# Click-rate tower on one core: adds and G products moved a tile back, gathers spread over four tiles, the last products regrouped

## The chip, the cores and the metric

The kernel runs on one core of a Trainium2 chip. TensorE (PE) multiplies, VectorE (DVE) and ScalarE (ACT) scale and add, GpSimd (POOL) builds small matrices and issues DMAs, SyncE (SP) only issues DMAs. The metric is the time of one execution on the device, in microseconds (us). Everything is fp32; the largest products are split into three products of rounded parts (hi and lo).

## What is computed

For 512 samples, 39 rows of 16 numbers are gathered from 39 tables. Three interaction layers of 128 rows follow, each summed over the 16 numbers, and then a small dense network:

```python
def _cin_layer(X0, Xi, W, b):
    Wr = W.reshape(H, F0_, Fi)
    return jnp.einsum('hjk,bjd,bkd->bhd', Wr, X0, Xi) + b[None, :, None]
X0 = embedded_features          # 512 x 39 x 16, the gathered rows
for W, b in Ws:                 # three layers
    Xi = _cin_layer(X0, Xi, W, b)
    res.append(Xi.sum(axis=2))
z = jnp.concatenate(res, axis=1)
h = jnp.concatenate([z, dense_ctx], axis=1)       # 3 x 128 + 16 = 400
h = jnp.maximum(h @ W_top1 + b_top1, 0.0)         # 512
h = jnp.maximum(h @ W_top2 + b_top2, 0.0)         # 256
y = h @ W_top3
```

## The kernel before

The 512 x 16 pairs of sample and number are 8192 columns. They are cut into 16 groups (0 to 15) of 512 columns (32 samples), and a group into 4 tiles of 128 columns; there are 64 tiles.

**The first layer of a group** is made one group ahead of its use. DVE multiplies rows of X0 (`form_pairs`, L653, seven times for a group, at chunk positions p = 6, 10, ... 30 of the group before) and PE multiplies these pairs with weights (`pair_product`, L394, five positions later, so at p = 11, 15, ... 35). PE also turns the group's X0 round (`transpose_x0`, L402, at p = 8, ahead of whose chunk it waits for the group's X0 to have been loaded). ACT adds the bias and rounds (L542, L551), DVE makes the rest (L660).

**The second layer** is the bulk of the work. For each tile PE makes ten chunks (`t_chunk`, three products each: L426, L427, L428; the tenth is narrower). ACT (L567) or DVE (L671) scales each chunk by the tile's column of X0 into `prod`. So a group has 40 positions p = 10 x tile + chunk. A tile's 24 slots of `prod` are then folded in half by an accumulating DMA of POOL (`fold`, L346), issued in the following tile, and DVE adds the rest in four steps (`sum_over_j`, L703) into x2, at chunks 1, 3, 5 and 7 of the tile that is BEHIND = 2 tiles later. One tile later again PE multiplies x2 with `diag` (`g_product`, L411), and ACT copies the result into G (`copy_g`, L556). POOL makes `diag` of each tile (`diagonal`, L334) once the tile before is scaled.

**The gathered rows** take a long way. POOL computes the indices of a group (`index`, L317) and issues ten indirect DMAs (`gather`, L324) into one half of `emb`. When all ten have landed, SP stores them to device memory (L245), waits, loads them as X0 (L255), waits, copies them inside SBUF (`rep`, L259, three DMAs), waits, and issues the loads of the factors that `form_pairs` multiplies (`factors`, L268 three DMAs, then L273 six). In its loop SP runs `factors(g)` and then `x0_of(g + 1)`. `factors(g)` is issued around the start of group g - 1, whose positions form the pairs of group g. So the store, load and copy of group g + 2 stand in group g, and its pairs are formed in group g + 1.

POOL's gathers of a group g + 2 are issued in program order between the folds. Before the change, nine of the ten stand in tiles 1 to 3 of group g - 1 and the tenth in tile 0 of group g.

**The end.** The last three G products follow the loop (tiles 61, 62, 63 of 0 to 63). Tile 63 has its fold on DVE (`fold_last`, L685). Between them stand the products of the first dense layer (`first_layer`, L471): four with `z0` of 128 rows and four with the 16 rows of dense_ctx, in turn. Then come nine products of the third layer (L491), four of `first_layer` with G, the split products (L502, L503, L505), and the rest of the dense network, which waits for the activation of z2 (L629).

## Time and profile before

| | us |
|---|---|
| median of 3 runs | 673.68 (673.07 to 673.69) |
| the profiled execution, its time | 672.67 |
| its span, from first to last instruction | 670.6 |
| PE busy in the span | 641.9 (96%) |
| DVE, ACT, POOL busy | 521.2, 488.3, 361.1 |
| mean granted clock of TensorE | 0.995 |

The profiled execution lies 1.0 us below the median of the runs, and 2.1 us of it lie outside the span. A group takes 36 us. Group 0 starts at 44.4 us, group 7 at 295.5 us, group 8 at 331.5 us, and the last tile ends at about 612 us; the rest is the end.

### The profile page before, as it was taken

Reading aid. Unit: us, or ns where it says so; the run is one execution under the profiler, and the core shown is the slowest. Engines: PE = TensorE matmul, PEld = TensorE weight load, DVE = VectorE, ACT = ScalarE, POOL = GpSimd, SP = SyncE. Lnnn points to the kernel's source line nnn. Section 1 sums busy time; section 2 is a strip of 40 time slices with the busy share of each in tenths; the row PEclk is TensorE's granted clock in tenths of the full one; section 3 lists DMA queues with packets and bytes.
Section 4 is the critical chain, followed back from the end, with each engine's and each line's share of the span. In section 5 each row is a group of like instructions: output and inputs, shape, how many; then the busy total and the mean of one; then the engine's idle time right before and its main releaser. Section 6 shows DMA issues by size and latency. Waiting matters only on the chain.

```text
span 670.6 us, 11899 instructions
## 1 busy us (share of the span) xinstructions
PE 641.9 (96%) x2516; PEld 461.4 (69%) x2516; DVE 521.2 (78%) x1478; ACT 488.3 (73%) x1692; POOL 361.1 (54%) x308
## 2 busy tenths in 40 slices
PE   0689999999999999999999999999999999999998
PEld 0246777777777777777777777777777777785483
DVE  0346888878888888888888878888888888897590
ACT  1137877778787868787877878787868787897293
POOL 6878766575656565755666675656575221121000
PEclk9799999999999999999999999999999999999999
DMA  6457687767676777667667767676777657567100
GB/s 225 60 92 168 112 183 133 173 131 162 124 160 128 159 150 163 142 134 155 139 144 134 167 130 161 124 160 129 160 150 162 142 102 178 126 122 215 31 1 0
DMA packets 61944, 91.05 MB, mean 136 GB/s; under 512 B 34599, under 2 KB 38548, under 8 KB 61671
## 3 DMA queue, kind: packets, MB, share of 16 engines
q0 software_dynamic: 14192, 51.02, 42.0%
q1 hardware_dynamic: 47734, 39.85, 21.2%
q8 instruction: 6, 0.10, 0.1%
q14 instruction: 12, 0.09, 0.0%
HBM read 10.59 MB, written 1.28 MB: 18 GB/s over the span
## 4 chain that ended last, share of the span: by engine, by line
PE 91%; POOL 3%; DMA 3%; issue 2%; SPq 1%; ACT 0%; DVE 0%; ACTq 0%; POOLq 0%
PE t_bank L426 22%; PE t_bank L427 21%; PE t_bank L428 21%; PE x_bank L394 14%; PE small_bank L411 5%; POOL emb L324 3%; PE t_bank L491 1%; PE t_bank L471 1%; PE t_bank L502 1%; PE t_bank L503 1%; PE t_bank L514 1%; PE t_bank L505 1%; DMA emb<-in_table,idx 1%; PE x0t_bank L402 1%; DMA emb_scratch<-emb 1%
## 5 line engine op out<-in xcount | busy, mean ns | idle before, releaser
L567 ACT ACTIVATE prod<-t_bank,x0t 128x128 f32<-128x128 f32 x1472 | 417.5, 377 | 114.6 <-PE t_bank L428 109.3
L671 DVE SCALAR_TENSOR_TENSOR prod<-t_bank,x0t,prod 128x128 f32<-128x128 f32 x1024 | 287.9, 343 | 80.1 <-PE t_bank L428 75.8
L426 PE MATMUL t_bank<-w_hi,x_hi 128*128 128x512 f32 (+1 forms) x640 | 307.5, 480 | 0.6 <-DVE x_lo L660 0.3
L427 PE MATMUL t_bank<-w_lo,x_hi 128*128 128x512 f32 (+1 forms) x640 | 247.8, 387 | 0.0
L428 PE MATMUL t_bank<-w_hi,x_lo 128*128 128x512 f32 (+1 forms) x640 | 247.0, 386 | 0.0
L324 POOL DMA_INDIRECT emb<-in_table,idx x160 | 211.8, 1324 | 48.5 <-issue 46.8
L334 POOL TENSOR_TENSOR diag<-x0t,mask 128x320 f32<-128x320 f32 x64 | 87.8, 1372 | 195.4 <-DVE prod L671 97.7
L426 PEld LDWEIGHTS t_bank<-w_hi,x_hi 128*128 128x128 f32 x640 | 120.2, 188 | 54.7 <-issue 29.7
L427 PEld LDWEIGHTS t_bank<-w_lo,x_hi 128*128 128x128 f32 x640 | 120.5, 188 | 47.1 <-issue 25.3
L428 PEld LDWEIGHTS t_bank<-w_hi,x_lo 128*128 128x128 f32 x640 | 120.1, 188 | 24.2
L703 DVE TENSOR_TENSOR prod<-prod 128x768 f32<-128x768 f32 (+2 forms) x192 | 117.4, 611 | 6.0 <-DMA prod<-prod 5.7
L394 PE MATMUL x_bank<-pairs,w_pair 117*128 117x512 f32 x224 | 114.6, 594 | 2.7 <-DVE pairs L653 1.9
L653 DVE TENSOR_TENSOR pairs<-shared 117x512 f32<-117x512 f32 x96 | 65.5, 682 | 6.8 <-DMA shared<-rep 6.8
L346 POOL DMA_DIRECT2D prod<-prod x63 | 60.5, 961 | 0.0
L394 PEld LDWEIGHTS x_bank<-pairs,w_pair 117*128 117x128 f32 x224 | 41.8, 190 | 15.6 <-DVE pairs L653 6.3
L411 PE MATMUL small_bank<-diag,x 128*128 128x320 f32 x128 | 45.0, 433 | 0.0
L556 ACT ACTIVATE G<-small_bank 128x320 f32 (+1 forms) x64 | 29.1, 454 | 4.8 <-PE small_bank L411 4.8
L448 PE MATMUL t_bank<-w_pair 117*128 117x512 f32 x20 | 13.2, 816 | 16.3 <-DVE w_pair L726 16.3
L411 PEld LDWEIGHTS small_bank<-diag,x 128*128 128x128 f32 x128 | 23.9, 188 | 6.8 <-issue 0.8
L534 ACT ACTIVATE x0t<-x0t_bank 128x39 f32<-128x39 f32 x64 | 13.8, 221 | 10.7 <-PE x0t_bank L402 9.2
L542 ACT ACTIVATE x<-x_bank,bias 128x512 f32<-128x512 f32 x16 | 11.4, 715 | 13.2 <-PE x_bank L394 13.2
L625 ACT ACTIVATE w_hi<-G 128x512 fp32r<-128x512 f32 x20 | 12.6, 632 | 11.5 <-PE t_bank L505 10.5
(73 smaller groups left out, 242.8 us busy)
## 6 DMA issues: line engine op xcount, KB each, us to landing
prod<-prod POOLq DMA_DIRECT2D x63, 768.0 KB, 7.1
shared<-rep SPq DMA_DIRECT2D x96, 234.0 KB
shared<-rep SPq DMA_DIRECT2D x48, 78.0 KB
emb<-in_table,idx POOLq DMA_INDIRECT x160
G<-in_w SPq DMA_DIRECT2D x1, 2496.0 KB
rep<-rep SPq DMA_DIRECT2D x28, 78.0 KB
rep<-emb_scratch SPq DMA_DIRECT2D x20, 78.0 KB
prod<-in_w SPq DMA_DIRECT2D x1, 1536.0 KB, 7.1
```

The source lines that it names most:

```text
L324: pool.indirect_dma_start(out=emb[:, half, i * D:(i + 1) * D], out_offset=None, in_=table, in_offset=bass.IndirectOffsetOnAxis(ap=idx[:, h ...
L334: pool.tensor_tensor(diag[:, slot, :, :], x0t[:, slot, :].unsqueeze(2).to_broadcast([P, J1, TB]), mask[:, :].unsqueeze(1).to_broadcast([P, ...
L346: pool.dma_start(prod[:, slot, 0:HALF, :].rearrange("p j h -> p (j h)"), prod[:, slot, HALF:, :].rearrange("p j h -> p (j h)"), accum_op=A ...
L394: pe.matmul(x1_bank[:, :], w_pair[:, b * H:(b + 1) * H], pairs[:, b % 2, :], start=b == 0, stop=b == BLOCKS - 1).then_inc(pair_mm, 1)
L411: pe.matmul(small_bank[:, 0:TB * J1], x2[:, slot % 2, :], diag[:, slot, :, :].rearrange("p j b -> p (j b)"), start=True, stop=True).then_i ...
L426: pe.matmul(acc, hi, w1_hi[:, cols], start=True, stop=False)
L427: pe.matmul(acc, hi, w1_lo[:, cols], start=False, stop=False)
L428: pe.matmul(acc, lo, w1_hi[:, cols], start=False, stop=True).then_inc(t_mm, 1)
L567: last = act.activation(prod[:, s, SLOT[c] + u, :], t_bank[c % T_BANKS][:, u * H:(u + 1) * H], ACT.Copy, scale=x0t[:, s, j:j + 1])
L653: dve.tensor_tensor(pairs[:, b % 2, :], first, rep[0:PAIRS, half, :] if b == 0 else second[:, k, :], ALU.mult).then_inc(pair_ready, 1)
L671: last = dve.scalar_tensor_tensor(unit, t_bank[c % T_BANKS][:, u * H:(u + 1) * H], x0t[:, s, j:j + 1], unit, ALU.mult, ALU.add)
L703: dve.tensor_tensor(out, left, right, ALU.add).then_inc(summed, 1)
```

## The change

BEHIND becomes 3: the adds of a tile come three tiles behind it and its G product four, now after chunk 0 of a tile (it was after chunk 2). In the last tile DVE adds two tiles (60 and 61), PE makes one more G product after chunk 7 (tile 60), and ACT copies it. After the loop tile 63 (folded by DVE) now comes ahead of tile 62 (folded by DMA). The ten gathers of group g + 2 now all stand in group g: 3, 3, 2 and 2 of them in its four tiles; those that were issued one group earlier are gone from there. The 16-row weights and dense_ctx are loaded into four strips of 32 partitions each, so SP issues eight small DMAs in place of two, and the four dense products use a tile position each and stand together between the last two G products. One product of `first_layer` with G moves behind the split products.

The core of the diff:

```diff
-BEHIND = 2
+BEHIND = 3
-GATHERS_EARLY = 9
-INDEX_TILE = 1
-G_AT = 2
+GATHERS_OF_TILE = [(0, 3), (3, 6), (6, 8), (8, GATHERS)]
+G_AT = 0
 G_COPY_AT = 5
+LAST_G_AT = 7
+LAST_G_COPY_AT = 9
...
-            sp.dma_start(wt1[0:D, 3, :], top1[3 * P:, :]).then_inc(wt1_loaded, 16)
-            sp.dma_start(dense[:, :], dense_t).then_inc(wt1_loaded, 16)
+            for m in range(M1):
+                strip = slice(m * STRIP, m * STRIP + D)
+                cols = slice(m * P, (m + 1) * P)
+                sp.dma_start(wt1[strip, 3, cols], top1[3 * P:, cols]).then_inc(wt1_loaded, 16)
+                sp.dma_start(dense[strip, :], dense_t).then_inc(wt1_loaded, 16)
...
-            index(AHEAD, 0)
-            for i in range(GATHERS_EARLY):
-                gather(i, 0)
-
-            def group(g, half, first=False, gathers=True, early=True):
+            def group(g, half, first=False, gathers=True):
                 for s in range(TILES_PER_GROUP):
                     t = g * TILES_PER_GROUP + s
-                    if early and s == INDEX_TILE:
-                        index(g + AHEAD + 1, 1 - half)
                     fold_before = not (first and s == 0)
+                    if gathers and s == 0:
+                        index(g + AHEAD, half)
                     if fold_before:
                         scaled(t - 1)
                     diagonal(t, s, first)
                     if fold_before:
                         fold((s - 1) % TILES_PER_GROUP)
-                    if gathers and s < INDEX_TILE:
-                        for i in range(GATHERS_EARLY, GATHERS):
+                    if gathers:
+                        for i in range(*GATHERS_OF_TILE[s]):
                             gather(i, half)
-                    if early and s >= INDEX_TILE:
-                        for i in range(3 * (s - INDEX_TILE), 3 * (s - INDEX_TILE) + 3):
-                            gather(i, 1 - half)
...
+                        if last and s == TILES_PER_GROUP - 1 and c == LAST_G_AT:
+                            g_product(t - BEHIND, 0)
...
-                if m == M1 - 1:
-                    g_product(TILES - 2, 2)
-                first_layer(m, P, 0, z0[:, :], start=True)
-                first_layer(m, D, 3, dense[:, :])
-            g_product(TILES - 1, 3)
+                first_layer(m, 0, z0[:, :], start=True)
+            pe.wait_ge(diag_ready, TILES)
+            g_product(TILES - 2, 3)
+            for m in range(M1):
+                strip = slice(m * STRIP, m * STRIP + D)
+                pe.matmul(h1_bank[m][:, :], wt1[strip, 3, m * P:(m + 1) * P], dense[strip, :],
+                          start=False, stop=False, tile_position=(m * STRIP, 0))
+            g_product(TILES - 1, 2)
...
-            for m in range(M1):
-                first_layer(m, P, 1, G[:, F, :])
+            for m in range(M1 - 1):
+                first_layer(m, 1, G[:, F, :])
...
+            first_layer(M1 - 1, 1, G[:, F, :])
             pe.wait_ge(z2_ready, 1)
...
-                        dve.wait_ge(g_mm, t - 1)
+                        dve.wait_ge(g_mm, min(t, TILES - 2) if isinstance(t, int) else t)
...
-            for i in range(RED):
-                sum_over_j(TILES - 2, GROUPS - 1, 2, i)
             fold_last(TILES - 1, 3)
             for i in range(RED):
-                sum_over_j(TILES - 1, GROUPS - 1, 3, i, by_dve=True)
+                sum_over_j(TILES - 2, GROUPS - 1, 3, i, by_dve=True)
+            for i in range(RED):
+                sum_over_j(TILES - 1, GROUPS - 1, 2, i)
```

POOL in group 13, the last one that issues gathers (they are those of group 15; `diag` is the tile's matrix, `prod<-prod` the fold of the tile before). Before:

```order
L334 TENSOR_TENSOR diag<-x0t,mask 128x320 [waits x0t_ready,g_mm,dve_scaled,act_scaled]
L346 DMA prod<-prod 128x1536
L324 DMA emb<-in_table,idx 125x16
L334 TENSOR_TENSOR diag<-x0t,mask 128x320 [waits x0t_ready,g_mm,dve_scaled,act_scaled]
L346 DMA prod<-prod 128x1536
```

The same place after the change, its four tiles:

```order
L339 TENSOR_TENSOR diag<-x0t,mask 128x320 [waits dve_scaled,x0t_ready,act_scaled,g_mm,emb_stored,index_ready]
L351 DMA prod<-prod 128x1536
L329 DMA emb<-in_table,idx 125x16 x3
L339 TENSOR_TENSOR diag<-x0t,mask 128x320 [waits x0t_ready,g_mm,dve_scaled,act_scaled]
L351 DMA prod<-prod 128x1536
L329 DMA emb<-in_table,idx 125x16 x3
L339 TENSOR_TENSOR diag<-x0t,mask 128x320 [waits x0t_ready,g_mm,dve_scaled,act_scaled]
L351 DMA prod<-prod 128x1536
L329 DMA emb<-in_table,idx 125x16 x2
L339 TENSOR_TENSOR diag<-x0t,mask 128x320 [waits x0t_ready,g_mm,dve_scaled,act_scaled]
L351 DMA prod<-prod 128x1536
L329 DMA emb<-in_table,idx 125x16 x2
```

The last gather of a group has moved from behind the fold of tile 0 to behind the fold of tile 3. The order on SP up to the end of the loop is unchanged.

PE behind the last chunk (`z` is z0, `dense` the 16 rows of dense_ctx, `small_bank<-diag` a G product). Before:

```order
L411 MATMUL small_bank<-diag,x 128x320 [waits g_copied,diag_ready,summed]
L471 MATMUL x_bank<-z,shared 128x512 [waits z0_ready,wt1_loaded]
L471 MATMUL x_bank<-dense,shared 128x512
L471 MATMUL x0t_bank<-z,shared 128x512
L471 MATMUL x0t_bank<-dense,shared 128x512
L471 MATMUL t_bank<-z,shared 128x512 [waits dve_scaled,act_scaled]
L471 MATMUL t_bank<-dense,shared 128x512
L411 MATMUL small_bank<-diag,x 128x320 [waits g_copied,diag_ready,summed]
L471 MATMUL t_bank<-z,shared 128x512
L471 MATMUL t_bank<-dense,shared 128x512
L411 MATMUL small_bank<-diag,x 128x320 [waits g_copied,diag_ready,summed]
```

After:

```order
L409 MATMUL small_bank<-diag,x 128x320 [waits g_copied,diag_ready,summed]
L471 MATMUL x_bank<-z,shared 128x512 [waits z0_ready,wt1_loaded]
L471 MATMUL x0t_bank<-z,shared 128x512
L471 MATMUL t_bank<-z,shared 128x512 [waits dve_scaled,act_scaled]
L471 MATMUL t_bank<-z,shared 128x512
L409 MATMUL small_bank<-diag,x 128x320 [waits diag_ready,g_copied,summed]
L485 MATMUL x_bank<-dense,shared 128x512
L485 MATMUL x0t_bank<-dense,shared 128x512
L485 MATMUL t_bank<-dense,shared 128x512 x2
L409 MATMUL small_bank<-diag,x 128x320 [waits g_copied,diag_ready,summed]
```

The four dense products have moved together, behind the G product that is last but one.

DVE from the second half of tile 63 (`prod<-prod` and `x<-prod` are adds, 128x1536 is the fold of tile 63). Before:

```order
L703 TENSOR_TENSOR x<-prod 128x128 [waits g_mm,summed]
L671 SCALAR_TENSOR_TENSOR prod<-t_bank,x0t,prod 128x128 [waits act_scaled,t_mm]
L671 SCALAR_TENSOR_TENSOR prod<-t_bank,x0t,prod 128x128 x3
L703 TENSOR_TENSOR prod<-prod 128x768 [waits folded2]
L703 TENSOR_TENSOR prod<-prod 128x384 [waits summed]
L703 TENSOR_TENSOR prod<-prod 128x128 [waits summed]
L703 TENSOR_TENSOR x<-prod 128x128 [waits g_mm,summed]
L685 TENSOR_TENSOR prod<-prod 128x1536 [waits dve_scaled,act_scaled]
L703 TENSOR_TENSOR prod<-prod 128x768 [waits last_folded]
```

After:

```order
L709 TENSOR_TENSOR x<-prod 128x128 [waits g_mm,summed]
L677 SCALAR_TENSOR_TENSOR prod<-t_bank,x0t,prod 128x128 [waits act_scaled,t_mm]
L677 SCALAR_TENSOR_TENSOR prod<-t_bank,x0t,prod 128x128 x3
L691 TENSOR_TENSOR prod<-prod 128x1536 [waits dve_scaled,act_scaled]
L709 TENSOR_TENSOR prod<-prod 128x768 [waits last_folded]
L709 TENSOR_TENSOR prod<-prod 128x384 [waits summed]
L709 TENSOR_TENSOR prod<-prod 128x128 [waits summed]
L709 TENSOR_TENSOR x<-prod 128x128 [waits g_mm,summed]
L709 TENSOR_TENSOR prod<-prod 128x768 [waits folded2]
```

DVE's own fold and the adds of tile 63 now stand ahead of the adds that wait for the folding DMA of tile 62.

## Rows read from the trace of the kernel before

**Rows 1.** A group: length; busy PE, PEld, DVE, ACT, POOL; clock; DMA share; GB/s.

```profile
305.00:341.00 36.00, 35.99 (x147) 26.75 (x147) 30.57 (x91) 28.48 (x105) 21.61 (x20) 1.00 0.70 146
```

**Rows 2.** Timeline of POOL, group 7: start, duration, engine, line, tile, count.

```profile
299.31 1.31 POOL L324 DMA_INDIRECT emb<-in_table,idx  x1 [0.30 <-issue]
...
325.19 0.99 POOL L346 DMA_DIRECT2D prod<-prod  x1
326.49 1.27 POOL L324 DMA_INDIRECT emb<-in_table,idx  x1 [0.30 <-issue]
328.05 1.22 POOL L324 DMA_INDIRECT emb<-in_table,idx  x1 [0.30 <-issue]
```

**Rows 3.** Timeline of SP's DMA issues, groups 6 to 8.

```profile
288.01 2.34 SPq L259 DMA_DIRECT2D rep<-rep  x3
294.06 2.38 SPq L268 DMA_DIRECT2D shared<-rep  x3
...
314.99 0.31 SPq L245 DMA_DIRECT2D emb_scratch<-emb  x1
317.91 0.34 SPq L255 DMA_DIRECT2D rep<-emb_scratch  x1
323.54 2.35 SPq L259 DMA_DIRECT2D rep<-rep  x3
327.22 4.08 SPq L268 DMA_DIRECT2D shared<-rep  x3
```

**Rows 4.** Timeline of PE in group 8: position 8, transposes, first pair product.

```profile
337.59 0.39 PE L426 MATMUL t_bank<-w_hi,x_hi 128*128 128x512 f32 x1
...
340.75 1.02 PE L394 MATMUL x_bank<-pairs,w_pair 117*128 117x512 f32 x2
```

**Rows 5.** The page's DMA issues: tile, queue, count, size, median us to landing.

```profile
prod<-prod POOLq DMA_DIRECT2D x63, 768.0 KB, 7.1
```

**Rows 6.** Chain that ended last, its pieces from gather to pair product at the start.

```profile
38.91 2.70 DMA emb<-in_table,idx
41.63 2.23 DMA emb_scratch<-emb
...
45.85 3.42 DMA rep<-emb_scratch
49.29 0.81 SPq L268
...
53.41 0.70 DVE pairs L653
```

**Rows 7.** Timeline of PE: its long idle time at the start, and the first pair product in group 0.

```profile
27.92 0.62 PE L402 MATMUL x0t_bank<-ident,rep 39*128 39x39 f32 x4 [5.49 <-DMA rep<-emb_scratch]
...
54.16 1.13 PE L394 MATMUL x_bank<-pairs,w_pair 117*128 117x512 f32 x2 [0.91 <-DVE pairs L653]
```

**Rows 8.** Busy time by stretch, around that idle time.

```profile
26.00:28.00 2.00, 0.08 (x1) 0.11 (x2) 0.00 (x0) 0.00 (x0) 1.41 (x2) 0.59 0.35 27
...
32.00:34.00 2.00, 2.00 (x5) 0.84 (x3) 1.27 (x2) 0.00 (x0) 1.65 (x2) 0.71 0.66 184
```

**Rows 9.** Timeline of DVE at the end.

```profile
607.33 1.12 DVE L671 SCALAR_TENSOR_TENSOR prod<-t_bank,x0t,prod 128x128 f32<-128x128 f32 x4 [0.61 <-PE t_bank L428]
...
615.53 1.88 DVE L703 TENSOR_TENSOR prod<-prod 128x768 f32<-128x768 f32 x3 [2.41 <-DMA prod<-prod]
...
617.65 1.75 DVE L685 TENSOR_TENSOR prod<-prod 128x1536 f32<-128x1536 f32 x1
```

**Rows 10.** Timeline of PE at the end.

```profile
618.02 1.12 PE L471 MATMUL t_bank<-dense,shared 16*128 16x512 f32 x2
619.07 0.81 PE L411 MATMUL small_bank<-diag,x 128*128 128x320 f32 x2
...
621.71 0.81 PE L411 MATMUL small_bank<-diag,x 128*128 128x320 f32 x2
...
655.97 1.12 PE L471 MATMUL x_bank<-prod,shared 128*128 128x512 f32 x2 [0.84 <-ACT prod L629]
```

32 lines of the change are left out of this document (20 added, 12 removed).

## The prediction

> **What bounds the kernel now.** I read the busy time by stretch first. In a middle group PE is busy 35.99 of 36.00 us at full clock, and no other engine comes near that [rows 1]. So the loop is a row of products without gaps: what another engine gains brings nothing, and what it loses costs something only once PE has to wait. The questions are whether the change adds, removes or delays a product. The list of waits shows that PE hardly waits between 45 us and 612 us; the end has gaps [rows 9, 10].
>
> The second view to read is the path of the gathered rows, since this is what the change moves most. It runs beside PE and appears nowhere as a wait: POOL issues ten gathers, they land, SP stores, loads, copies, loads factors, DVE forms the pair, PE multiplies it. For group 9: the last gather is issued at 299.31 in tile 0 of group 7 [rows 2]. SP stores only at 314.99, because it comes to it only then, after the factors of group 8. It loads at 317.91, copies at 323.54, and issues the factors at 327.22 [rows 3]. PE needs them in group 8: it starts position 8 (which waits for the X0 copies) at 337.59 and the first pair product at 340.75 [rows 4]. So today the gathers have 15.7 us to spare ahead of the store (314.99 - 299.31), and the rest of the path some 10 us ahead of position 8 (337.59 - 327.22).
>
> **The gathers.** In the changed order the last two gathers of group 9 stand behind the fold in tile 3 of group 7, so where 326.49 and 328.05 stand in the rows [rows 2]. That is 28.7 us later than 299.31, and the slack in front of the store was 15.7 us. Now the store waits for them. I work out when the first pair product can start, step by step.
>
> - Landing. A gather took 2.70 us with little beside it [rows 6], which gives 328.05 + 2.70 = 330.75. But the fold issued at 325.19 is ahead of it in POOL's own DMA queue, and a fold lands 7.1 us after its issue [rows 2, 5], so at 332.3. Lower bound 330.75; I take 332.3, since the gathers stand behind that fold.
> - Store to load: 2.92 us in this group (314.99 to 317.91), 2.23 at the start [rows 3, 6]. I take 2.92, the row of a loop under load.
> - Load to copies: 5.63 us (317.91 to 323.54) against 3.42 from issue to landing of the load at the start, where no fold was under way [rows 3, 6]. I take 5.63: a fold is issued 1 to 3 us before the load in both places.
> - Copies to factors: 3.68 us (323.54 to 327.22), and 6.05 one group before (288.01 to 294.06) [rows 3]. I take 3.68, because PE stands still by then and no further fold is issued.
> - Factors to form 4.12 us (49.29 to 53.41), form to pair product 0.75 (53.41 to 54.16) [rows 6, 7]. In the loop this leg has slack, so the start is the only row for it.
>
> The copies have landed at 332.3 + 2.92 + 5.63 + 3.68 = 344.5, and the pair product starts at 344.5 + 4.12 + 0.75 = 349.4. Before it was 340.75. PE waits 8.65 us in this group: first at position 8, from 337.6 to 344.5, and then a second time at the pair product, since from position 8 it has 3.2 us of work (340.75 - 337.59). With the low values (330.75 + 2.23 + 3.42 + 3.68 + 4.87) it is 345.0, a wait of 4.2; with 6.05 for the copies 351.8, a wait of 11.0.
>
> Behind SP's store wait stand its own load, copies and the factors of the same group, nothing else. Behind DVE's wait for the factors stand the last add, chunk 8 and the next chunks, so banks run full too; PE is already waiting. The wait is paid anew in each group: PE's work from the last gather to the pair product stays 12.7 us (328.05 to 340.75), and the path stays 21.35 us. Groups 2 to 15 are gathered this way, so there are 14 such waits.
>
> **The clock.** PE was idle for 5.49 us before 27.92 [rows 7]. In 26 to 28 us the granted clock is 0.59, in 32 to 34 it is 0.71, between these 0.50 [rows 8]. From these means it fell at 26.35, 3.9 us into the idle time, and rose at 33.15, 5.2 us after PE had work again: 6.8 us at 1.2 GHz. The new wait at position 8 is 6.9 us, so the clock will fall there too, at about 341.5, and rise at about 348.3. By then PE has done 1.9 of its 3.16 us, and it reaches the pair product at 349.55, 0.15 us late. If it rises only 6.3 us after work starts, at 350.85, it is 1.45 us late. I take 0.15, so 8.8 us for a group: the clock's loss hides in the second wait. The Trainium skill (TensorE: Matmul & The Clock Gate, "HAM oscillation — how this bites in real kernels") says that a kernel which waits for a DMA in each round falls back to half clock in each round. This is the rule that speaks most against this change, and the rows on the idle time at the start agree with it.
>
> **G products a tile later, after chunk 0.** The number of products is unchanged (64), and each keeps its length. The adds now wait for a fold that was issued a whole tile earlier, so these waits go; off the path, nothing. The last add of a tile ends close to the end of that tile, and chunk 0 gives about 0.7 us of PE work behind it, so the G product finds it ready. I count nothing; a miss of 0.3 us in all 52 tiles of the loop would be 15 us, inside the range.
>
> **The end.** DVE waited 2.41 us for the fold of tile 62 and started its adds at 615.53, so it had been free since 613.12. Four adds take 2.12 us (615.53 to 617.65), the own fold 1.79 with the gap behind it (to 619.44), and four more adds end at 621.56 [rows 9]. Now four more adds lie in tile 63, of which at least the idle 0.61 us absorbs a part [rows 9] (and 0.3 more of a like gap): free at 614.3, then 1.79 + 2.12 + 2.12 gives 620.35, 1.2 us earlier. But the dense products now stand between the last two G products. A 16-row product took 1.05 us from its start to the next one's (618.02 to 619.07) [rows 10]. Tile 63's adds end at 618.2, its G product takes 0.65, four dense products in a row 4.2: the last G product starts at 623.05, where it was 621.71 [rows 10], so 1.35 later. The product moved behind the split ones fills the 0.84 us in which PE waited for z2 [rows 10]. Together +0.5 us. No row shows two products at once, so this sum goes by the row. The Trainium skill (TensorEngine Tiling (Array Packing), "Key Properties") says that tiles of the array work independently and in parallel. By that rule the four dense products would take little more than one and the end would come out at 1.2 + 0.84, about 2.0 us faster. The eight small DMAs of SP are issued some 30 us before they are needed; nothing. At the start nine gathers fewer stand ahead of the first `diag`; at most the 0.91 us that PE waited at 54.16 [rows 7], counted as nothing.
>
> **Sum.** Against the profiled execution: 672.67 + 14 x 8.8 + 0.5 = 796.4. The median of the runs is 1.0 above that execution, so **797 us**.
>
> **Rivals.**
> - *The path has room after all* (other side): the last gather is early enough, as the spare 15.7 and 10 us suggest at first sight. It decides at a path of 12.7 us from the last gather's issue to the pair product, against 21.35 by my legs; even the low ones give 16.9. Then only the end and the start count: 673.7 - 2.0 (dense products overlapping) = 671.7, or 674.2 with them in a row. For it: nothing in the profile but the size of my legs under load. 6%.
> - *The load isn't held back by the fold.* I read the 5.63 us against 3.42 as a load that waits behind a fold. The load now comes close to the start of the next fold and may be ahead of it. Each wait is then 2.2 us shorter: 14 x 6.6 + 0.5 gives 766. The Trainium skill (DMA: Bandwidth & Descriptors, "Queues, rings and completion order") says that each DMA engine goes round its queues packet by packet, by which a load would share with a fold and not wait for its end. The 5.63 us speak against that, the chance below stands for it. 14%.
> - *The clock isn't hidden.* If PE is at half clock for the whole 6.8 us in which it has work, each group costs 3.4 us more: 797 + 14 x 3.25, about 843. It needs a clock that falls late in the wait. 12%.
> - *My sum*, waits of 6.9 to 11 us: 770 to 828, 68%.
>
> **How the numbers follow.** The likeliest gives 797. The range must take in the low and high ends of the legs: 14 x 4.2 + 673.7 = 732 and 14 x 11.0 + 14 x 1.45 + 674 = 848. I set 735 to 848; outside it lie the first rival and little else. A measurement of this kernel can tell 0.2% (1.35 us) from no change. Faster by more than that: 3%, the half of the first rival with overlapping dense products; within it 2%; slower 95%.
>
> **What the profile after would show.** If right: the length of a group is 43 to 47 us in place of 36; PE's list of waits has about 14 waits for the X0 load (released by the DMA `rep<-rep`) and about 14 for DVE's pairs; DVE waits for `shared<-rep`; SP's store comes at the very end of tile 3 or in the next tile 0, 3 to 5 us after the last gather's issue; the clock row shows dips. The last group and the end look as before to within 2 us. If the groups are still 36 us long, the path is shorter than I summed, and the prediction fails at the legs from landing to factors. If they are longer than 48 us, the clock or a leg that grows with the wait is at work.

## The result, and the profile after

The changed kernel takes **810.43 us** (median of 6 runs, 809.10 to 814.06) where the kernel before takes 673.68 (6 runs, 673.07 to 677.39). The ratio is 1.203, with a 95% interval from 1.199 to 1.206. The profiled execution took 809.83 us, its span is 808.0, the mean granted clock 0.922. The prediction was 797, with a range of 735 to 848.

The page of the kernel after. First the span, then from its second part PE's busy tenths and its granted clock in 40 slices:

```profile
span 808.0 us, 11899 instructions
...
PE   2699796979969696988969696996969697899898
...
PEclk9899897998979898998979898898979899799999
```

PE has gaps all through the loop now, and the clock row has a dip for about every group. The list of waits (engine, line, what for: us in total, times, longest) names them:

```profile
DVE pairs L659 <- DMA shared<-rep: 147.4, 19, 9.9
...
PE t_bank L424 <- DMA rep<-rep: 98.1, 14, 7.4
```

Fourteen times PE waits at position 8 for the X0 copies, on average 7.0 us (98.1 / 14). Group 8 shows the whole path. POOL's fold and last gather, then SP's DMA issues (start, duration, engine and line, tile, count), the lines that answer to [rows 2, 3]:

```profile
392.82 1.02 POOL L351 DMA_DIRECT2D prod<-prod  x1
...
395.72 1.21 POOL L329 DMA_INDIRECT emb<-in_table,idx  x1 [0.30 <-issue]
```

```profile
399.76 0.31 SPq L247 DMA_DIRECT2D emb_scratch<-emb  x1
402.18 0.34 SPq L257 DMA_DIRECT2D rep<-emb_scratch  x1
408.90 2.35 SPq L261 DMA_DIRECT2D rep<-rep  x3
412.53 2.38 SPq L270 DMA_DIRECT2D shared<-rep  x3
```

Before, the last gather stood 15.7 us ahead of the store. Now the store comes 4.04 us behind it, as soon as the gather has landed. DVE (form of the pair, add) and PE (position 8, G product, first pair product), which answer to [rows 4]:

```profile
416.64 0.69 DVE L659 TENSOR_TENSOR pairs<-shared,rep 117x512 f32<-117x512 f32 x1 [9.87 <-DMA shared<-rep]
417.25 0.28 DVE L709 TENSOR_TENSOR x<-prod 128x128 f32<-128x128 f32 x1
```

```profile
412.74 0.79 PE L424 MATMUL t_bank<-w_hi,x_hi 128*128 128x512 f32 x1 [7.36 <-DMA rep<-rep]
...
417.59 1.43 PE L409 MATMUL small_bank<-diag,x 128*128 128x320 f32 x2
...
419.60 1.02 PE L392 MATMUL x_bank<-pairs,w_pair 117*128 117x512 f32 x2
```

From position 8 to the pair product PE had 3.16 us of work before (337.59 to 340.75); here 6.86 us pass. The busy time by stretch tells why. The columns are those of [rows 1]: length; busy PE, PEld, DVE, ACT, POOL; clock; DMA share; GB/s. The first line is the whole group.

```profile
399.00:445.70 46.70, 39.20 (x147) 28.32 (x146) 30.10 (x92) 28.58 (x105) 20.92 (x19) 0.89 0.53 112
...
408.00:410.00 2.00, 0.00 (x0) 0.00 (x0) 0.00 (x0) 0.00 (x0) 0.00 (x0) 0.69 0.04 5
410.00:412.00 2.00, 0.00 (x0) 0.00 (x0) 0.00 (x0) 0.00 (x0) 0.00 (x0) 0.50 0.31 84
412.00:416.00 4.00, 3.26 (x10) 2.44 (x11) 0.00 (x0) 0.00 (x0) 0.00 (x0) 0.50 0.21 60
416.00:418.00 2.00, 1.90 (x5) 1.08 (x5) 1.36 (x5) 1.19 (x5) 0.00 (x0) 0.50 0.61 196
418.00:420.00 2.00, 2.00 (x6) 1.28 (x6) 2.00 (x5) 1.12 (x6) 0.88 (x1) 0.75 0.50 166
```

PE fell idle at 405.38 (412.74 - 7.36). By the means of the stretches it was granted half clock (1.2 of 2.4 GHz) from about 408.8, 3.4 us into the idle time, to about 419.0, 6.3 us after it had work again.

Group 8 is one of the longer groups; longer and shorter ones come in turn. Group 9 has the clock back after 4.3 us of work (at about 463.4, from 459.11), and its pair product starts 2.3 us behind DVE's form (463.02 to 465.30), where group 8 has 2.96:

```profile
462.00:464.00 2.00, 1.73 (x6) 1.08 (x5) 0.98 (x3) 0.94 (x4) 0.00 (x0) 0.66 0.57 179
```

```profile
463.96 0.81 PE L409 MATMUL small_bank<-diag,x 128*128 128x320 f32 x2 [0.27 <-DVE x L709]
...
465.30 1.02 PE L392 MATMUL x_bank<-pairs,w_pair 117*128 117x512 f32 x2
```

Behind group 1 (43.7 us) the groups take 45.4 to 45.8 us and 46.3 to 46.6 us in turn. From the form to the pair product the 14 groups have 2.29 to 3.09 us, 2.58 on average.

In the whole program: group 1 starts at 79.55 us and group 15 at 721.96, where they started at 79.71 and 583.15. So 14 groups cost 138.97 us more, **9.93 each** (predicted 8.8). The start is 0.16 us shorter, and group 15 with the end takes 86.04 in place of 87.45, 1.41 less. Together 137.4, the difference of the spans.

The end of PE, which answers to [rows 10]:

```profile
758.33 0.69 PE L485 MATMUL x_bank<-dense,shared 16*128 16x512 f32 x1
758.34 0.69 PE L485 MATMUL x0t_bank<-dense,shared 16*128 16x512 f32 x1
758.34 0.70 PE L485 MATMUL t_bank<-dense,shared 16*128 16x512 f32 x2
758.86 0.59 PE L485 MATMUL x_bank<-dense,shared 16*128 16x512 f32 x1
...
759.96 0.78 PE L409 MATMUL small_bank<-diag,x 128*128 128x320 f32 x2 [0.49 <-ACT G L560]
761.26 4.13 PE L494 MATMUL t_bank<-G,prod 128*128 128x512 f32 x9 [0.53 <-ACT G L560]
```

The four dense products start within 0.01 us of one another and are done 1.1 us later (758.86 + 0.59 = 759.45); one alone took 1.05 before.

### The profile page after: what moved, and what is told of

The parts are those of the page before. It is cut to its first block, busy times and chain, and to the rows that moved or that the text cites. A ratio compares the mean times of both kernels' runs of the same rounds, so it can differ in the third digit from the quotient of the medians.

```text
span 808.0 us, 11899 instructions
## 1 busy us (share of the span) xinstructions
PE 676.3 (84%) x2516; PEld 479.4 (59%) x2516; DVE 515.7 (64%) x1478; ACT 489.9 (61%) x1692; POOL 344.2 (43%) x308
## 4 chain that ended last, share of the span: by engine, by line
PE 48%; DMA 32%; POOL 6%; SPq 6%; issue 4%; DVE 1%; ACT 1%; DVEq 0%; POOLq 0%; ACTq 0%
DMA rep<-emb_scratch 11%; PE t_bank L424 10%; PE t_bank L425 10%; PE t_bank L426 10%; PE x_bank L392 8%; DMA emb<-in_table,idx 7%; DMA shared<-rep 5%; PE small_bank L409 4%; DMA emb_scratch<-emb 4%; POOL emb L329 4%; DMA rep<-rep 4%; SPq L261 3%; SPq L270 3%; POOL diag L339 2%; DMA prod<-in_w 1%
## 5 line engine op out<-in xcount | busy, mean ns | idle before, releaser
L424 PE MATMUL t_bank<-w_hi,x_hi 128*128 128x512 f32 (+1 forms) x640 | 321.3, 502 | 98.7 <-DMA rep<-rep 98.1
L425 PE MATMUL t_bank<-w_lo,x_hi 128*128 128x512 f32 (+1 forms) x640 | 256.5, 401 | 0.0
L426 PE MATMUL t_bank<-w_hi,x_lo 128*128 128x512 f32 (+1 forms) x640 | 254.5, 398 | 0.0
L339 POOL TENSOR_TENSOR diag<-x0t,mask 128x320 f32<-128x320 f32 x64 | 74.3, 1162 | 350.5 <-PE small_bank L409 241.4
L329 POOL DMA_INDIRECT emb<-in_table,idx x160 | 202.9, 1268 | 48.4 <-issue 47.5
L424 PEld LDWEIGHTS t_bank<-w_hi,x_hi 128*128 128x128 f32 x640 | 125.9, 197 | 159.0 <-issue 129.4
L425 PEld LDWEIGHTS t_bank<-w_lo,x_hi 128*128 128x128 f32 x640 | 126.9, 198 | 46.8 <-issue 26.2
L426 PEld LDWEIGHTS t_bank<-w_hi,x_lo 128*128 128x128 f32 x640 | 126.0, 197 | 25.7
L659 DVE TENSOR_TENSOR pairs<-shared,rep 117x512 f32<-117x512 f32 x16 | 11.1, 693 | 143.5 <-DMA shared<-rep 143.5
L409 PE MATMUL small_bank<-diag,x 128*128 128x320 f32 x128 | 50.4, 478 | 5.1 <-DVE x L709 2.4
L538 ACT ACTIVATE x0t<-x0t_bank 128x39 f32<-128x39 f32 x64 | 13.6, 218 | 11.2 <-PE x0t_bank L400 10.9
```

The lines of the kernel that those rows point to most:

```text
L329: pool.indirect_dma_start(out=emb[:, half, i * D:(i + 1) * D], out_offset=None, in_=table, in_offset=bass.IndirectOffsetOnAxis(ap=idx[:, h ...
L339: pool.tensor_tensor(diag[:, slot, :, :], x0t[:, slot, :].unsqueeze(2).to_broadcast([P, J1, TB]), mask[:, :].unsqueeze(1).to_broadcast([P, ...
L409: pe.matmul(small_bank[:, 0:TB * J1], x2[:, slot % 2, :], diag[:, slot, :, :].rearrange("p j b -> p (j b)"), start=True, stop=True).then_i ...
L424: pe.matmul(acc, hi, w1_hi[:, cols], start=True, stop=False)
L425: pe.matmul(acc, hi, w1_lo[:, cols], start=False, stop=False)
L426: pe.matmul(acc, lo, w1_hi[:, cols], start=False, stop=True).then_inc(t_mm, 1)
```

## The experiments

My theory was that the gathers alone make the loss, by a path of DMAs that has become longer than PE's work beside it, and that the half clock adds to it. The rivals: the other parts cost something themselves; the load isn't held back by the fold; the clock is hidden, or costs in full. The table gives what was measured; "per group" is the time from the start of group 1 to that of group 15, over 14, less 35.96. The runs with the late gathers (e2, e3, e4, e5, e7, e10 and e11) were executed once each, those near 674 us 12 times; the six executions of the kernel after lie between 809.1 and 814.1. So single times are compared to a few microseconds, and the rows of the traces carry the rest.

| run | us | per group, us | clock |
|---|---|---|---|
| before | 673.68 | 0 | 0.995 |
| after | 810.43 | 9.93 | 0.922 |
| e1_gathers_back | 674.58 | 0.22 | 0.995 |
| e2_gathers_alone | 804.17 | 9.39 | 0.928 |
| e3_gathers_tile2 | 697.81 | 1.95 | 0.988 |
| e4_busy_gathers_alone | 791.99 | 8.56 | 0.996 |
| e5_small_fold | 783.12 | 8.12 | 0.937 |
| e7_changed_g2 | 834.45 | 11.64 | 0.910 |
| e10_tile2_old_adds | 702.28 | 1.90 | 0.978 |
| e11_busy_changed | 817.63 | 10.54 | 0.979 |
| e6_end_alone | 674.47 | 0 | 0.990 |
| e6_best_g2 | 674.43 | 0 | 0.992 |
| e9_warm_end | 672.58 | 0 | 0.995 |
| e12_mixed | 671.75 | 0 | 0.992 |

**Which part it is: the gathers taken back.** The changed kernel with POOL's order of before:

```diff
-GATHERS_OF_TILE = [(0, 3), (3, 6), (6, 8), (8, GATHERS)]
+GATHERS_EARLY = 9
+INDEX_TILE = 1
...
```

> The changed kernel with the gathers of before (nine of ten a group ahead, the tenth in tile 0); adds, G products, strips and the end stay changed. Theory (the late gathers are the whole slowdown): groups of 36.0 us again, the end about 2 us shorter than before (dense products overlap, adds of the last tiles earlier, a product fills the 0.84 us wait), so 671 to 672.5 us. Rival (the later adds and G products cost a good part, since G products wait up to 0.45 us for DVE's last add in the changed trace): groups stay longer than 36.3 us and the time is above 678.

Measured: 674.58 us beside 673.11 for the kernel before, ratio 1.0023 (1.0000 to 1.0046). The loss of 137 us is gone, so no other part can make it without the gathers. But the time is 2.1 to 3.6 us above my expectation. The end is 1.5 us shorter, and the gain is eaten by one wait for DVE in group 1, tile 1, at the G product that now comes after chunk 0:

```profile
90.79 0.81 PE L417 MATMUL small_bank<-diag,x 128*128 128x320 f32 x2 [2.76 <-DVE x L717]
```

**And the gathers alone.** The kernel before with POOL's new order and nothing else (the same lines, with the signs turned).

> The kernel before with only its gathers moved to 3, 3, 2, 2 in the four tiles of the group. Theory: the whole slowdown, groups of about 46 us and 808 to 815 us. Rival (adds and G products share in it): below 790.

Measured: 804.17 us, 4 below the range that I had expected and 131 above the 673.11 of before in the same set, so the gathers alone make 131 of the 137 us. The wait is the same one (list of waits):

```profile
PE t_bank L418 <- DMA rep<-rep: 96.4, 14, 8.1
```

The 6 us that are left are 14 x (9.93 - 9.39) = 7.6 us in the loop, less the 1.4 us gained at the end. The 0.54 us a group come at the pair product. Over the 14 groups it starts on average 1.48 us behind the form here and 2.58 us in the kernel after, 1.1 us later. About 0.55 us of these are the G product itself (that is what one takes at full clock in the chain of the kernel after, at 390.78), which here follows the pair product and there stands ahead of it. The rest is its wait for the add that DVE makes behind the form, and the half clock that it meets. In group 8 the two are 1.93 (416.04 to 417.97) and 2.96 us.

**How far the last gather may move.** The changed kernel with the last gathers in tile 2:

```diff
-GATHERS_OF_TILE = [(0, 3), (3, 6), (6, 8), (8, GATHERS)]
+GATHERS_OF_TILE = [(0, 4), (4, 7), (7, GATHERS), (0, 0)]
```

> The changed kernel with its gathers in tiles 0 to 2 (4, 3, 3, 0), so that the last is issued one tile (some 9.4 us) earlier. Theory (a path of fixed length that starts at the last gather): the wait of 7.4 us at position 8 is gone or under 1 us, no fall of the clock, 671 to 690 us. Rival (the waits come from DMA load in tile 0 or from the sheer number of gathers in a group, wherever they stand): the groups stay over 43 us, above 780.

Measured: 697.81 us, above the range of 671 to 690. Hardly a wait for the X0 copies is left. The rival (the number of gathers in a group makes the waits) is out: they are the same ten here. PE waits for DVE's add at the G product instead (list of waits), and each group is 1.95 us longer:

```profile
PE small_bank L409 <- DVE x L709: 19.7, 13, 4.1
```

I took this for a meeting of two edits: the late form stands ahead of the add, and the G product after chunk 0 has no work to cover it. The next run tested that, with the same gathers and the adds of before.

> The kernel before with the spread gathers alone, 4, 3 and 3 in tiles 0, 1 and 2, none in tile 3. In e3_gathers_tile2 the same gathers with the new adds gave 697.8, with PE waiting 19.7 us at the G product after chunk 0. Theory: that loss is the meeting of two edits (the late form stands ahead of the add, and the G product waits for the add with no PE work behind it); with the old adds the form may be as late and nothing waits: 672 to 678, no wait for the X0 copies, list of waits for DVE's add nearly empty, groups 36.0 to 36.3. Rival: a late form costs by itself, at the pair product: 690 to 700.

Measured: 702.28 us, and 1.90 us a group. My forecast (nothing waits, 672 to 678) was wrong, and the rival holds: a late form costs by itself. It is lost at the pair product, in about every second group. SP and PE for group 7 (the last gather was issued at 296.83):

```profile
299.60 0.30 SPq L244 DMA_DIRECT2D emb_scratch<-emb  x1
301.92 0.34 SPq L254 DMA_DIRECT2D rep<-emb_scratch  x1
308.36 2.34 SPq L258 DMA_DIRECT2D rep<-rep  x3
312.08 4.05 SPq L267 DMA_DIRECT2D shared<-rep  x3
```

```profile
319.01 1.87 PE L386 MATMUL x_bank<-pairs,w_pair 117*128 117x512 f32 x2 [2.04 <-DVE pairs L645]
```

From the last gather to the pair product pass 22.2 us (319.01 - 296.83), of which PE waits 2.04, so its own work there is 20.1. The path is a little too long even from tile 2. It fits where its legs are quick: the load takes 6.44 us here, issued 0.71 us behind a fold (301.21). In group 9 it is issued 0.66 us ahead of the fold (377.45 and 378.11), takes 2.63 us, and PE doesn't wait. In group 8 it takes 2.95, but then the factors take 8.26 (348.62 to 356.88), and PE waits 0.75. So this is the same mechanism with a smaller deficit.

What decides is how the load meets the fold. In the 14 groups of this run the load takes 2.6 to 3.0 us where it is issued ahead of the fold or less than 0.1 us behind it (7 groups), and 5.7 to 6.4 us where it is issued 0.3 us or more behind it (7 groups). The other runs with late gathers and a whole fold agree: up to 0.2 us behind the fold at most 3.0 us, from 0.3 to 2.2 us behind it at least 5.7.

Nor is the wait all that a group loses. Group 7 takes 39.91 us, 3.95 more than 35.96, for a wait of 2.04; behind it PE is at half clock for a while:

```profile
320.00:322.00 2.00, 2.00 (x6) 1.20 (x5) 1.66 (x3) 1.24 (x5) 1.56 (x1) 0.50 0.33 119
```

That the two runs lose the same per group is no sign of one cause. In e3_gathers_tile2 the load is quick in 11 of the 14 groups, and these still take 37.1 us on average; in this run the groups with a quick load take 36.2. So the meeting costs about 0.9 us in such a group, and this run has more groups with a slow load instead.

The 4.5 us between the two runs' totals lie at the end: e10 takes 90.6 us from the start of group 15, with the end of before, where the kernel before takes 87.45. In it the clock fell while PE was never idle; the kernel before has the same products there at 1.00:

```profile
644.00:648.00 4.00, 4.00 (x6) 1.29 (x5) 3.86 (x6) 0.00 (x0) 0.00 (x0) 0.50 0.01 6
```

**What the half clock costs.** The kernel of e2_gathers_alone with idle work in the wait, eight products of about 0.86 us:

```diff
+BUSY = 8
...
+                if not (first_tile and c < T_BANKS):
+                    pe.wait_ge(*scaled_before(t, c))
+                if then_x0t is not None and BUSY and not first_group:
+                    for _ in range(BUSY):
+                        pe.matmul(t_bank[c % T_BANKS][:, :], w_pair[:, 0:P], w_pair[:, 0:COLS], start=True, stop=True)
                 if then_x0t is not None:
...
```

> The kernel before with the gathers alone changed (804.17 us), and in each of the 14 waits at position 8 eight idle products (0.86 us each, 6.9 us, into the bank that the chunk overwrites anyway) ahead of the wait for the X0 copies. Nothing else. Theory: the wait is unchanged, but the clock stays at full rate, so PE reaches the pair product at once and waits there for DVE's pair (form at 416.04 + 0.75 = 416.8, where it was 417.97): 1.2 us less in each group, about 787. Rival (the clock's loss is hidden, as predicted): 802 to 806. Second rival (PE's 3.4 us at half rate count in full): 755 to 760.

Measured: 791.99 us, 12.2 less than without, 0.83 us a group; I had expected 787. The clock stays at 1.00, and PE has time left in front of the pair product (1.2 to 1.3 us in most groups), as my prediction had said of it:

```profile
PE x_bank L387 <- DVE pairs L649: 17.5, 17, 1.3
```

So the half clock costs 0.83 us a group there: neither nothing (802 to 806) nor all of its 3.4 us (755 to 760). Without it the deficit of a group is 8.56 us, and my legs had given 8.65. The same in the changed kernel:

> The changed kernel with eight idle products of about 0.86 us in front of the X0 transposes of every group but the first, so that PE works through the wait (as e4_busy_gathers_alone did on the kernel before with the gathers alone, 804.2 to 792.0). Theory: the clock's share is the same, 12 us of the 137: 796 to 800, mean clock above 0.99, the pair product 1 us after the form. Rival: with the G product after chunk 0 the clock costs more (the pair product came 2.96 us after the form, not 1.93): 785 to 793.

Measured: 817.63 us, 7 us **more** than without the idle products (and 3.6 more than the longest of the six executions without them); both expectations are wrong. PE now comes early to the G product and waits there for DVE's add, 14 times and 29.4 us in all. In eight of the 14 groups the clock falls at the end of this wait or up to 1.5 us behind it, with PE's work still ahead (PE in group 8, and the stretch behind it):

```profile
420.69 1.33 PE L410 MATMUL small_bank<-diag,x 128*128 128x320 f32 x2 [2.21 <-DVE x L713]
```

```profile
422.00:424.00 2.00, 2.00 (x6) 1.19 (x5) 1.14 (x2) 0.66 (x3) 1.89 (x2) 0.50 0.27 94
```

A wait of the same length does not always bring this. In group 11 of the same run the clock stays at 1.00:

```profile
562.52 0.81 PE L410 MATMUL small_bank<-diag,x 128*128 128x320 f32 x2 [2.21 <-DVE x L713]
```

```profile
562.00:564.00 2.00, 1.48 (x6) 1.20 (x7) 2.00 (x7) 1.24 (x5) 0.25 (x1) 1.00 0.72 227
```

So idle work at one wait can move the drop to the next one, and the length of that one does not decide it alone. From group 2 on tile 1 takes 13.6 us where the clock fell and 11.9 where it didn't (10.4 to 11.3 in the kernel after). The difference, 1.64 us, eight times is 13.1 us, 0.94 a group. Without it this run would have 9.60 us a group in place of 10.54. By this estimate the clock costs the changed kernel about 0.3 us a group (9.93 less 9.60), and the early G product about 1.0 us at full clock (9.60 less the 8.56 of e4_busy_gathers_alone). Group 11 shows the second one: the form starts at 561.57 and the pair product at 563.86, 2.29 us behind it at full clock, where e4 has 0.75.

**Does the fold hold the load back?** The changed kernel, with the fold ahead of the load cut to 16 of 128 partitions:

```diff
+                rows = 16 if slot == TILES_PER_GROUP - 1 else P
-                pool.dma_start(prod[:, slot, 0:HALF, :].rearrange("p j h -> p (j h)"),
-                               prod[:, slot, HALF:, :].rearrange("p j h -> p (j h)"),
+                pool.dma_start(prod[0:rows, slot, 0:HALF, :].rearrange("p j h -> p (j h)"),
+                               prod[0:rows, slot, HALF:, :].rearrange("p j h -> p (j h)"),
```

> The changed kernel with the folding DMA that is issued in tile 0 (that of slot 3) cut to 16 of its 128 partitions, so that 112 partitions of tile 3's second half are left out of the sums; everything else stays. Theory: the X0 load shares its time with this fold (6.7 us from issue to the copies' issue, against 3.4 at the start), so it falls to about 3.5, the wait at position 8 from 7.3 to about 4 us, and the clock falls later or not at all: 750 to 768 us. Rival (the load's length is its own, 1248 pieces of 64 bytes): 805 to 812.

Measured: 783.12 us, 27 less. The load, in SP's rows, takes 4.27 us from its issue to the copies (6.72 in the kernel after):

```profile
390.88 0.33 SPq L257 DMA_DIRECT2D rep<-emb_scratch  x1
395.15 2.35 SPq L261 DMA_DIRECT2D rep<-rep  x3
```

So the fold holds the load back: by 2.4 us in this group, and by 2.0 on average over the 14 (6.3 to 4.3). It isn't the whole of it: I had expected 3.5 us and 750 to 768, and a load that is issued ahead of the whole fold takes less than this one, 2.6 to 3.0. And only 1.8 us come out in a group (9.93 to 8.12): the idle time is still 4.86 us in group 8, the clock still falls, and it rises later relative to the form, which starts 3.23 us ahead of the pair product there (2.3 to 3.25 in all).

**Why the G product has to come early.** The changed kernel with G_AT = 2, as before:

```diff
-G_AT = 0
+G_AT = 2
```

> The changed kernel, only the G products after chunk 2 as before. The changed kernel took 810, the kernel with the gathers alone 804. Theory: the 6 us between them come from the G product after chunk 0 of tile 1, which waits for an add that DVE makes behind its wait for the factors, 0.3 to 0.4 us and 0.5 us at half rate in each group: 802 to 805. Rival (the later adds themselves): 808 to 812.

Measured: 834.45 us; wrong in sign. I had looked only at PE's and DVE's side of the G product. POOL's `diag` of a tile waits for the G product four tiles back, and the fold and the gathers stand behind it in POOL's order. In tile 3 it now starts 3.8 us into the tile (1.6 in the kernel after). POOL in group 7, `diag` of tile 3 and the last gather:

```profile
405.57 0.73 POOL L339 TENSOR_TENSOR diag<-x0t,mask 128x320 f32<-128x320 f32 x1 [5.18 <-PE small_bank L409]
...
409.15 1.21 POOL L329 DMA_INDIRECT emb<-in_table,idx  x1 [0.30 <-issue]
```

Group 8 starts at 410.94 here, so the last gather is issued 1.8 us ahead of it; in the kernel after it is 3.4 (395.72 and 399.08). That is 1.6 us later, and each group is 1.71 longer (11.64 less 9.93), 24 us in all. It agrees with the path from the other side: what delays the last gather delays each group by about as much. It is not an exact measure, since the pair product also stands ahead of the G product here and starts 1.9 us behind the form, not 2.58.

**The end by itself.** The kernel before with the regrouped end (strips, the dense products together, one product moved behind the split ones), without the adds that come later:

```diff
...
-                if m == M1 - 1:
-                    g_product(TILES - 2, 2)
-                first_layer(m, P, 0, z0[:, :], start=True)
-                first_layer(m, D, 3, dense[:, :])
+                first_layer(m, 0, z0[:, :], start=True)
+            g_product(TILES - 2, 2)
+            for m in range(M1):
+                strip = slice(m * STRIP, m * STRIP + D)
+                pe.matmul(h1_bank[m][:, :], wt1[strip, 3, m * P:(m + 1) * P], dense[strip, :],
+                          start=False, stop=False, tile_position=(m * STRIP, 0))
             g_product(TILES - 1, 3)
...
```

> The kernel before with the end's regrouping alone: strips with tile positions, the four dense products together ahead of the last G product, one product behind the split ones; adds two tiles behind as before. Theory: DVE's adds still end where they did, so the last G product is not earlier; the filled wait gives 0.8 us: 672.6 to 673.2. Rival (dense products were on the path): 671 or less.

Measured: 674.47 us, ratio 1.0014 (0.9999 to 1.0029): no gain, and 1.3 us above the expected range. The dense products do run side by side, but then PE has nothing to do until DVE's adds are done:

```profile
617.48 0.81 PE L415 MATMUL small_bank<-diag,x 128*128 128x320 f32 x2 [1.07 <-DVE x L710]
...
621.38 1.44 PE L415 MATMUL small_bank<-diag,x 128*128 128x320 f32 x2 [2.03 <-DVE x L710]
```

```profile
620.00:622.00 2.00, 0.61 (x1) 0.50 (x2) 1.90 (x5) 0.00 (x0) 0.00 (x0) 0.79 0.00 0
622.00:624.00 2.00, 1.47 (x3) 0.50 (x2) 2.00 (x3) 1.11 (x3) 0.00 (x0) 0.50 0.72 182
```

and the clock falls, until 628: the third layer's nine products take 10.27 us where they took 7.99. The 3.1 us that the products save turn into a wait, and the wait costs the clock.

**Is there a version that beats the kernel before?** The gathers of before with all the rest of the change, and three settings of the G product and of PE's work at the end. First G_AT = 2 throughout:

> The changed kernel with the gathers of before, and the G products after chunk 2 as before (not after chunk 0); adds three tiles behind and the changed end stay. In the run with the gathers back PE waited 2.8 us for DVE's last add in group 1, since the G product stood right behind chunk 0. Theory: that wait goes, the end stays 1.5 us shorter than before, so about 2 us below that run: 671 to 672.5, against 673.1 for the kernel before. Rival (the position of the G products is of no account): 673.5 to 675.

Measured: 674.43 us, ratio 1.0005 (0.9980 to 1.0029). It is 2 to 3.5 us above what I expected. The wait in group 1 is gone, but the last G product waits 1.64 us for ACT's copy, and the clock is 0.50 in 624 to 626. Then the same with idle products there:

```diff
+KEEP = [0, 3, 1]
...
+            fill(KEEP[1])
             g_product(TILES - 1, 2)
...
+            fill(KEEP[2])
             pe.wait_ge(g_copied, TILES)
```

> The kernel of e6_best_g2 (gathers of before, three and four tiles behind, G product after chunk 2, dense strips, swapped last tiles) with four idle products of 0.43 us at the end: three between the dense products and the last G product, where PE waited 1.64 us for ACT, and one ahead of the wait for the copied G (0.53 us). They write a bank that is overwritten next. Theory: in e6_best_g2 the clock fell (0.57 in 623:627) because PE did little from 619.2 on, and the third layer took 9.69 us for 18 products where it took 7.99 before; kept busy, PE stays at 1.00, the third layer takes 8.0 and the end is 1.5 to 2 us shorter: span 669 to 669.8, median 672 to 673, faster than before by 0.1 to 0.25%. Rival: the clock falls for another reason (the narrow rows of the dense products): still below 0.7 there, span 671, no gain.

Measured: 672.58 us, ratio 0.9989 (0.9961 to 1.0018). The clock is 1.00 in every stretch from 614 to 632, so with the narrow products still there, filling the waits was enough to keep it up, as the theory said; as a gain it can't be told from none. Last, G_AT = 2 except in the last group:

```diff
+G_AT = 2
+LAST_GROUP_G_AT = 0
...
-                        if c == G_AT and not (first and s <= BEHIND):
+                        if c == (LAST_GROUP_G_AT if last else G_AT) and not (first and s <= BEHIND):
```

> The gathers of before, the rest as in the changed kernel, but the G product after chunk 2 in every group except the last and after chunk 0 in the last. e1_gathers_back (after chunk 0 everywhere) had an end 1.5 us shorter than before, paid for by a wait of 2.8 us in group 1; e6_best_g2 (after chunk 2 everywhere) had no such wait, but the long end. Theory: both gains add, since the wait belongs to group 1 and the short end to the last group: no wait for DVE's add in group 1, groups 36.0, the clock 1.00 through the end, 64.0 to 64.3 us from the start of tile 63 to the end of the span; with a start 0.5 to 1.0 us later than before the span is 669.3 to 670.3, the median 671.8 to 672.6, ratio 0.998 to 0.999. Rival: the rigid place costs in the last group too, or the clock falls at the end: 673.5 to 675.

Measured: 671.75 us beside 673.21, ratio 0.9978 (0.9954 to 1.0001). Its profiled execution has the span of the theory, 669.3, and the full clock over the end:

```profile
622.00:624.00 2.00, 1.47 (x4) 0.68 (x4) 2.00 (x2) 1.84 (x4) 0.00 (x0) 1.00 0.66 214
```

Group 15 with the end takes 85.9 us (87.45 before), and the start 0.2 more. Its 12 runs fall into two sets, six from 669.9 to 671.1 and six from 672.4 to 675.6. A drop of the clock at the end that comes in some executions would do that. It is not shown: the mean clock of the six longer ones is 0.990 to 0.995 and that of the others 0.992 to 0.995, and the kernel before spreads as widely in the same set, from 672.4 to 677.1. It is the fastest median of the study, and its interval just includes no change.

## Why the prediction was right, and where its terms were off

**The mechanism** is the one predicted: the last gather behind the fold in tile 3, the store waiting for it, PE waiting 14 times for the X0 copies, DVE for its factors. e2_gathers_alone shows it alone, e1_gathers_back shows the rest without it, e7_changed_g2 moves the last gather 1.6 us later and each group grows by 1.7; with the last gather one tile earlier (e3, e10) hardly a wait for the X0 copies is left. One sign failed: I had expected about 14 waits of PE for DVE's pairs, and the list has three, 2.7 us in all. The pair product comes late by PE's own queue instead, as told below.

**The legs.** Last gather to store: 4.25 predicted, 4.04 measured. Store to load 2.92, measured 2.42. Load to copies 5.63, measured 6.72 in this group; 6.3 to 6.7 in 13 of the groups and 3.0 in group 1. Copies to factors 3.68, measured 3.63. Together 16.48 to 16.81. The wait at position 8 came out at 6.9 predicted, 7.0 measured. The last gather lands just behind the fold ahead of it: by the trace the fold lands at 399.00, 6.2 us after its issue (I had used 7.1), and the gather at 399.54. The largest miss among these is the load under a fold, 1.1 us; the quicker store makes up for half of it. Factors to form: 4.12 predicted, 4.11 measured.

From the last gather to the form that is 20.60 us predicted and 20.64 on average. Such a fit is in part luck: on average the landing was 0.2 and the store 0.5 us too long, the load 0.7 too short. And that the load is the slow kind hangs on little, since it is issued 0.4 to 0.6 us behind the fold, and loads up to 0.2 us behind one were quick.

**What was off lies between the form and the pair product,** and two terms share it. I had 0.90 us there (0.75, and 0.15 for the clock); measured are 2.58 on average. Of the 1.68 us more, about 0.55 are the G product's own time, which no longer follows behind; the rest is the 9.93 - 8.8 = 1.13 us by which I missed a group. That is 14 x 1.13 = 15.8 us; the end takes 1.9 of them back, and the error of the whole is 13.4.

The first term is the G products after chunk 0, which I had costed at nothing, on PE's side alone ("the G product finds it ready"). In tile 1 it doesn't: DVE is behind as well, and makes the last add only after the form (417.25 behind 416.64). So the G product waits for the add, and chunk 1 and the pair product stand behind it. Even at full clock the pair product then starts 2.29 us behind the form (e11_busy_changed, group 11). Where the gathers are early, this order costs one wait of 2.8 us in group 1 and nothing in the other groups.

The second is the clock. I had it hidden: full rate again 5.2 us after PE had work, a second wait at the pair product, 0.15 us left. It fell 3.4 us into the idle time in group 8 and 4.5 in group 9 (predicted 3.9), and rose 6.3 and 4.3 us after the work began; the text had named the later rise as an open end. In group 8 it slowed the G product too.

How the loss divides depends on which term is taken first. Without both it is 8.56 us a group (e4). The clock alone adds 0.83 (9.39, e2), and the G product on top of it 0.54 (9.93, after). The other way round the G product adds about 1.0 and the clock about 0.3, by the estimate from e11. Either way both are well above what I had put, 0 and 0.15, and the range held them. The Trainium skill (TensorE: Matmul & The Clock Gate, "HAM oscillation — how this bites in real kernels") had the direction: half clock in each round with a wait for a DMA, and the trace agrees, 0.50 between 410 and 418.

**The end** I had at +0.5 us; it is -1.4. The dense products run together (1.1 us, not 4.2), so the last G product starts 16.20 us after tile 63 (before 16.66) and not 1.35 us later; the moved product fills the wait for z2, 0.85 us (predicted 0.84); 0.1 comes in the tiles. The rule that I had set beside my sum (the Trainium skill, TensorEngine Tiling (Array Packing), "Key Properties", independent tiles in parallel) is right here, with 0.01 us between the four starts.

**The rivals.** "The path has room" is out: the room is 12.7 us, and e10 shows that even 20.1 us are not enough. "The load isn't held back" is out for 13 of the 14 groups, by e5_small_fold. Its condition, a load at the start of the fold, was met in group 1: issued 0.2 us behind the fold, the load took 3.0 us. Its rule (the Trainium skill, DMA: Bandwidth & Descriptors, "Queues, rings and completion order": the engines go round their queues packet by packet) isn't refuted by the measurements: behind a small fold the load still took 4.27 us and behind a whole one 6.3 to 6.7, so it grows with what is under way. No run shows why 0.1 us in the order of the two issues makes 3 us. "The clock isn't hidden" was right in kind and not in size: 0.3 to 0.8 us a group and not 3.4.

## What to carry to other kernels

A DMA chain of several hops that appears nowhere as a wait has to be added up, hop by hop under the load that it will meet, against the busy engine's work beside it, before its first link is moved; here it needs 17 us to the copies and nearly 22 to the product, and once PE waits for it, a later first link comes out nearly one to one in each round. Work that needs another engine's late result should not stand ahead of the next critical product: here the G product did, and cost about 1 us a group at full clock, and its wait can bring the clock down as well. And work saved in front of a wait is a gain only if something else moves into its place: at the end of this kernel four products run in the time of one, and in e6_end_alone PE then waited and lost its clock.

## What I had not expected of the hardware

- Four fp32 products with 16 rows each, in four strips of the array, took 1.1 us together (758.33 to 759.45), against 1.05 us from one to the next when they were issued alone between wide ones.
- The length of an idle time does not by itself say whether the clock falls. It fell at 1.07 and 2.03 us with the strip products between them (e6_end_alone), at 1.64 and 0.53 at the end of e6_best_g2, at 2.04 in e10 and at 2.21 in group 8 of e11. It stayed at 1.00 with 1.32 (e4) and 1.39 us (at the end of the kernel after), but also with 2.21 in group 11 of e11 and with 2.18 in group 5 of e10:

```profile
244.77 1.13 PE L386 MATMUL x_bank<-pairs,w_pair 117*128 117x512 f32 x2 [2.18 <-DVE pairs L645]
```

```profile
244.00:248.00 4.00, 3.23 (x12) 2.27 (x13) 3.97 (x11) 1.36 (x6) 1.80 (x2) 1.00 0.41 127
```

- It also fell in 644 to 648 of e10_tile2_old_adds with PE busy 4.00 of 4.00 us, in a stretch with only six records of products, two of them with 16 rows. In the kernel before the same products ran at 1.00. What made the difference stays open.
- In e10_tile2_old_adds the same load took 2.63 us to the next step when it was issued 0.66 us ahead of a fold, and 6.44 when it was issued 0.71 us behind one. The switch is narrow: over all runs with late gathers and a whole fold, a load up to 0.2 us behind it took at most 3.0 us and one 0.3 to 2.2 us behind it at least 5.7. So a tenth of a microsecond in the order of two issues on different queues moved the smaller transfer's end by about 3 us.
